# Four LayerNorm and weight-loading stages of a two-layer transformer block, with tile t's normalisation issued after tile t+1's statistics and loads issued further ahead

## The reference, cut to what matters

```
xn = layernorm(x)                                  # no weight, eps 1e-5
x  = x + L0_attn(xn) + L0_ffn(xn)                  # L0_ffn adds its own input xn, and
                                                   # begins with layernorm(xn) * norm_w + norm_b
xn = layernorm(x)
x  = x + L1_attn(xn) + L1_ffn(xn)

def L1_ffn(x):                                     # x_prev is x moved down by one token
    xr = mu_r * x + (1 - mu_r) * x_prev
    xk = mu_k * x + (1 - mu_k) * x_prev
    return sigmoid(xr @ W_r.T) * (relu(xk @ W_k.T) ** 2 @ W_v.T)
```

## Time and profile before

| what | value |
|---|---|
| time before, median of 3 runs | 15645.25 us (15638.21 to 15674.76) |
| the profiled execution's own time | 15637.75 us |
| its span, first to last instruction, slowest core | 15636.2 us |
| spans of the eight cores | 15612.7 to 15636.2 us |
| granted TensorE clock, mean of a core | 0.594 to 0.596 of full speed |
| busy: PE, ACT, DVE | 65%, 30%, 27% of the span |

### The profile page before, as it was taken

How to read it: one execution, slowest core, us unless ns; L and a number is a source line. 1 busy time by engine, 2 the same in 40 slices (tenths; PEclk the granted TensorE clock), 3 DMA queues, 4 the chain that set the end, 5 groups by cost and what they waited for, 6 DMA issues and landing times.

```text
span 15636.2 us, 129774 instructions; the slowest of 8 cores (15612.7 to 15636.2 us)
## 1 busy us (share of the span) xinstructions
...
## 2 busy tenths in 40 slices
...
DMA packets 113302, 335.26 MB, mean 21 GB/s; under 512 B 17082, under 2 KB 37115, under 8 KB 111358
## 3 DMA queue, kind: packets, MB, share of 16 engines
...
## 4 chain that ended last, share of the span: by engine, by line
PE 60%; DVE 22%; issue 8%; DMA 6%; ACT 3%; DVEq 1%; SPq 0%; ACTq 0%; POOL 0%; POOLq 0%; PEldq 0%
PE l_PS L1355 9%; PE l_PAV L1330 7%; PE l_PSM L1339 7%; PE l0a_PAV L522 5%; PE l0a_PS L541 5%; PE l0f_PS L930 3%; PE l0f_PSM L912 3%; PE l0f_PAV L901 3%; PE l0a_PQ L333 1%; DVE l0a_recip L573 1%; DVE l_recip L1387 1%; DVE l0f_rrow L956 1%; PE l_PO L1414 1%; PE l0a_PO L602 1%; DMA as_f<-f 1%
## 5 line engine op out<-in xcount | busy, mean ns | idle before, releaser
L1364 ACT ACTIVATE l_PT<-l_PS,l_cb 128x1024 bf16<-128x1024 f32 x2048 | 2281.9, 1114 | 2174.1 <-PE l_PS L1355 2160.4
L547 ACT ACTIVATE l0a_PTexp<-l0a_PS,l0a_cb 128x1024 bf16<-128x1024 f32 x1152 | 1284.6, 1115 | 1152.2 <-PE l0a_PS L541 1146.3
L1355 PE MATMUL l_PS<-l_qw,l_kT 64*128 64x512 bf16 x4096 | 1630.4, 591 | 5.8 <-DMA l_qw<-qT1f 5.8
L1330 PE MATMUL l_PAV<-l_PT,l_V 128*64 128x512 bf16 x4096 | 1309.1, 633 | 414.4 <-DVE l_PAV L1319 389.6
L939 ACT ACTIVATE l0f_PT<-l0f_PS,l0f_cb 128x1536 bf16<-128x1536 f32 (+1 forms) x704 | 1057.7, 1502 | 1124.4 <-PE l0f_PS L930 1118.3
L1339 PE MATMUL l_PSM<-l_PT,cs_onescol_bf 128*1 128x512 bf16 x4096 | 1208.9, 586 | 0.0
L522 PE MATMUL l0a_PAV<-l0a_PTexp,l0a_V 128*33 128x512 bf16 x2304 | 855.9, 586 | 540.4 <-DVE l0a_PAV L511 298.9
L1374 DVE COPY l_pavc<-l_PAV 128x512 f32<-128x512 f32 x64 | 44.3, 692 | 3695.6 <-PE l_PSM L1339 3695.6
L541 PE MATMUL l0a_PS<-l0a_qT_all,l0a_kT_all 32*128 32x512 bf16 x2304 | 913.3, 592 | 2.3 <-POOLq L98 2.3
L930 PE MATMUL l0f_PS<-l0f_qw,l0f_kTh 128*128 128x512 bf16 x2048 | 659.5, 443 | 7.1 <-DMA l0f_kTh<-kT0f 7.1
L901 PE MATMUL l0f_PAV<-l0f_PT,l0f_V 128*128 128x512 bf16 x2048 | 591.4, 398 | 48.7 <-ACT l0f_PT L939 48.1
...
...
## 6 DMA issues: line engine op xcount, KB each, us to landing
ln_x_x<-x SPq DMA_DIRECT2D x32, 512.0 KB, 3.2
a<-l0a_obuf POOLq DMA_DIRECT2D x32, 512.0 KB, 4.4
x<-x SPq DMA_DIRECT2D x32, 512.0 KB, 3.3
f<-l0f_zbuf POOLq DMA_DIRECT2D x32, 512.0 KB, 26.2
as_x<-x SPq DMA_DIRECT2D x32, 512.0 KB, 3.9
as_a<-a SPq DMA_DIRECT2D x32, 512.0 KB, 4.7
as_f<-f SPq DMA_DIRECT2D x32, 512.0 KB
x<-as_x1f POOLq DMA_DIRECT2D x32, 512.0 KB, 3.2
```

Of the source, the lines that this page charges most:

```text
L547: exp_t = b.act(lambda e, bb=bb: e.activation(PT[:, 1024 * bb:1024 * bb + 1024], PS[:, 1024 * bb:1024 * bb + 1024], AF.Exp, bias=cb[:], sc ...
L1330: b.pe(lambda e, kt=kt, g=g, ii=ii, bb=bb, last=last: e.matmul(PAV[64 * ii:64 * ii + 64, :], V1[:, 256 * kt + 64 * g:256 * kt + 64 * g + 6 ...
L1355: pe_s = b.pe(lambda e, kt=kt, v=v, ii=ii, bb=bb, qb_=qb_: e.matmul(PS[:, 1024 * bb + 512 * ii:1024 * bb + 512 * ii + 512], kT64[v][64 * i ...
L1364: exp_t = b.act(lambda e, bb=bb: e.activation(PT[:, 1024 * bb:1024 * bb + 1024], PS[:, 1024 * bb:1024 * bb + 1024], AF.Exp, bias=cb[:], sc ...
```

## The change

1. In all three LayerNorm loops the body is split in two. A step `tl` of 33 issues the load and the statistics of tile `tl` (with ACT's Ln and Exp), and then normalisation, transposes and copy-out of tile `tl - 1`. The small `mv` tile (and `rst2`, `xnf` in `emit_xn2T`) has two copies for it.
2. `emit_xn2T` has four x buffers, and a load waits for the first reader of the tile that last held the buffer.
3. `emit_assembly_ln` keeps two buffers per tensor, but a load waits for the last reader of that same buffer, two tiles before.
4. `wload` stages through four buffers (`x1s` and `a1s`) on semaphores ld4 to ld7.

No operation on data is added or removed. The core of the diff (`emit_ln_xnT` is split as the assembly is; in `emit_xn2T` the second half is the second `tensor_scalar`, the two `tensor_tensor` with weight and bias, transposes and copy-out):

```diff
 def emit_xn2T(...):
-    xs = [b.sb(f"x2_{i}", [128, D], F32, es) for i in range(2)]
-    xnf = b.sb("x2_xnf", [128, D], F32, es)
+    xs = [b.sb(f"x2_{i}", [128, D], F32, es) for i in range(4)]
+    xnfs = [b.sb(f"x2_xnf{i}", [128, D], F32, es) for i in range(2)]
...
-            waits=[("ve", ve_done)] if t >= 2 else (), slot=buf)
-        b.ve(lambda e, t=t, buf=buf: e.tensor_scalar(
-            xnf[:], xs[buf][:], stats_sb[:, 2 * t:2 * t + 1],
+                waits=[("ve", scal_hist[buf])] if t >= 4 else (), slot=buf)
+            scal_hist[buf] = b.ve(lambda e, t=t, buf=buf, nb2=nb2: e.tensor_scalar(
+                xnfs[nb2][:], xs[buf][:], stats_sb[:, 2 * t:2 * t + 1],
...
 def emit_assembly_ln(...):
-    mv = b.sb("as_mv", [128, 2], F32, es)
+    mvs = [b.sb(f"as_mv{i}", [128, 2], F32, es) for i in range(2)]
...
-    for t in range(NT):
-        buf = t % 2
-        w0 = [("ve", ve_done)] if t >= 2 else ()
+    scal_hist = [b.cnt["ve"], b.cnt["ve"]]
+    ars = {}
+    for tl in range(NT + 1):
+        if tl < NT:
+            t, buf, nb = tl, tl % 2, tl % 2
+            w0 = [("ve", scal_hist[buf])] if t >= 2 else ()
...
+            scal_hist[buf] = b.ve(lambda e, buf=buf, x1f=x1f: e.tensor_tensor(
+                x1f[:], x1f[:], xs[buf][:], OP.add), waits=[l1])
+            if add_xn:
+                scal_hist[buf] = b.ve(lambda e, t=t, buf=buf: e.tensor_scalar(
+                    tmp[:], xs[buf][:], stats_sb[:, 2 * t:2 * t + 1],
+                    stats_sb[:, 2 * t + 1:2 * t + 2], OP.subtract, OP.mult))
...
-        a_r = b.act(lambda e, t=t: e.activation(
-            stats1_sb[:, 2 * t + 1:2 * t + 2], lnv[:], AF.Exp, bias=0.0, scale=-0.5))
-        ve_done = b.ve(lambda e, t=t, x1f=x1f: e.tensor_scalar(
-            xnb[t % 2][:], x1f[:], stats1_sb[:, 2 * t:2 * t + 1],
-            stats1_sb[:, 2 * t + 1:2 * t + 2], OP.subtract, OP.mult),
-            waits=[("act", a_r), ("pe", pe_done)])
+            ars[t] = b.act(lambda e, t=t: e.activation(
+                stats1_sb[:, 2 * t + 1:2 * t + 2], lnv[:], AF.Exp, bias=0.0,
+                scale=-0.5))
+        if tl >= 1:
+            t, nb = tl - 1, (tl - 1) % 2
+            x1f = x1fs[nb]
+            ve_done = b.ve(lambda e, t=t, nb=nb, x1f=x1f: e.tensor_scalar(
+                xnb[nb][:], x1f[:], stats1_sb[:, 2 * t:2 * t + 1],
+                stats1_sb[:, 2 * t + 1:2 * t + 2], OP.subtract, OP.mult),
+                waits=[("act", ars.pop(t)), ("pe", pe_done)])
...
 def emit_l1ffn_final(...):
-    castc = [b.cnt["ve"], b.cnt["ve"]]
+    castc = [b.cnt["ve"]] * 4
+    wstages = [x1s[0], x1s[1], a1s[0], a1s[1]]
...
-            sbf = c % 2
+            sbf = c % 4
             ld = b.ld(lambda e, c=c, sbf=sbf, cap=cap: e.dma_start(
-                out=x1s[sbf][:], in_=cap[128 * c:128 * c + 128, :]),
-                waits=[("ve", castc[sbf])], slot=6 + sbf)
+                out=wstages[sbf][:], in_=cap[128 * c:128 * c + 128, :]),
+                waits=[("ve", castc[sbf])], slot=4 + sbf)
```

More of the change, by code:

```diff
@@ L162, in emit_ln_xnT @@
     st6 = b.sb(f"ln_st6_{tag}", [128, 12], F32, es)
-    mv = b.sb(f"ln_mv_{tag}", [128, 2], F32, es)
+    mvs = [b.sb(f"ln_mv{i}_{tag}", [128, 2], F32, es) for i in range(2)]
     lnv = b.sb(f"ln_lnv_{tag}", [128, 1], F32, es)
@@ L171, in emit_ln_xnT @@
             b.ve(lambda e, c=c: e.memset(xnT[c][:, 0:1], 0.0), inc="ve")
-    ve_done = b.cnt["ve"]
     pe_done = b.cnt["pe"]
@@ L176, in emit_ln_xnT @@
     scal_hist = [b.cnt["ve"]] * 4
-    for t in range(NT):
[L178 to L216, removed]
-            for c in range(NC):
[L218 to L222, removed]
@@ L635, in emit_xn2T @@
     es = b.scope()
-    xs = [b.sb(f"x2_{i}", [128, D], F32, es) for i in range(2)]
-    xnf = b.sb("x2_xnf", [128, D], F32, es)
+    xs = [b.sb(f"x2_{i}", [128, D], F32, es) for i in range(4)]
+    xnfs = [b.sb(f"x2_xnf{i}", [128, D], F32, es) for i in range(2)]
     st6 = b.sb("x2_st6", [128, 12], F32, es)
-    mv = b.sb("x2_mv", [128, 2], F32, es)
+    mvs = [b.sb(f"x2_mv{i}", [128, 2], F32, es) for i in range(2)]
     lnv = b.sb("x2_lnv", [128, 1], F32, es)
-    rst2 = b.sb("x2_rst2", [128, 1], F32, es)
+    rsts = [b.sb(f"x2_rst2{i}", [128, 1], F32, es) for i in range(2)]
     xnb = [b.sb(f"x2_xnb{i}", [128, D], BF16, es) for i in range(2)]
@@ L667, in emit_xn2T @@
     vv = b.ve(lambda e: e.tensor_copy(bbc[:], PB[:]), waits=[("pe", pv)])
-    ve_done = b.cnt["ve"]
     pe_done = b.cnt["pe"]
     evac_cnt = [b.cnt["ve"], b.cnt["ve"]]
-    for t in range(NT):
-        buf = t % 2
-        ld_t = b.ld(lambda e, t=t, buf=buf: e.dma_start(
-            out=xs[buf][:], in_=x_dram[128 * t:128 * t + 128, :]),
-            waits=[("ve", ve_done)] if t >= 2 else (), slot=buf)
-        b.ve(lambda e, t=t, buf=buf: e.tensor_scalar(
-            xnf[:], xs[buf][:], stats_sb[:, 2 * t:2 * t + 1],
[L679 to L706, removed]
@@ new lines, in emit_xn2T @@
+    scal_hist = [b.cnt["ve"]] * 4
+    ars = {}
+    for tl in range(NT + 1):
+        if tl < NT:
+            t, buf, nb2 = tl, tl % 4, tl % 2
+            ld_t = b.ld(lambda e, t=t, buf=buf: e.dma_start(
+                out=xs[buf][:], in_=x_dram[128 * t:128 * t + 128, :]),
+                waits=[("ve", scal_hist[buf])] if t >= 4 else (), slot=buf)
+            scal_hist[buf] = b.ve(lambda e, t=t, buf=buf, nb2=nb2: e.tensor_scalar(
+                xnfs[nb2][:], xs[buf][:], stats_sb[:, 2 * t:2 * t + 1],
+                stats_sb[:, 2 * t + 1:2 * t + 2], OP.subtract, OP.mult),
+                waits=[ld_t])
+            s1 = b.ve(lambda e, nb2=nb2: e.bn_stats(st6[:, 0:6], xnfs[nb2][:, 0:512]))
+            s2 = b.ve(lambda e, nb2=nb2: e.bn_stats(st6[:, 6:12], xnfs[nb2][:, 512:1024]),
+                      waits=[("ve", s1)])
+            ve_mv = b.ve(lambda e, nb2=nb2: e.bn_aggr(mvs[nb2][:], st6[:]),
+                         waits=[("ve", s2)])
+            b.act(lambda e, nb2=nb2: e.activation(lnv[:], mvs[nb2][:, 1:2], AF.Ln,
+                                                  bias=eps5[:], scale=1.0),
+                  waits=[("ve", ve_mv)])
+            ars[t] = b.act(lambda e, nb2=nb2: e.activation(
+                rsts[nb2][:], lnv[:], AF.Exp, bias=0.0, scale=-0.5))
+        if tl >= 1:
+            t, nb2 = tl - 1, (tl - 1) % 2
+            b.ve(lambda e, nb2=nb2: e.tensor_scalar(
+                xnfs[nb2][:], xnfs[nb2][:], mvs[nb2][:, 0:1], rsts[nb2][:],
+                OP.subtract, OP.mult),
+                waits=[("act", ars.pop(t))])
+            b.ve(lambda e, nb2=nb2: e.tensor_tensor(xnfs[nb2][:], xnfs[nb2][:],
+                                                    wbc[:], OP.mult))
+            ve_done = b.ve(lambda e, nb2=nb2: e.tensor_tensor(
+                xnb[nb2][:], xnfs[nb2][:], bbc[:], OP.add),
+                waits=[("pe", pe_done)])
+            pb = t % 2
+            tp = None
+            for c in range(NC):
+                w2 = [("ve", ve_done), ("ve", evac_cnt[pb])] if c == 0 else ()
+                tp = b.pe(lambda e, c=c, nb2=nb2, pb=pb: e.transpose(
+                    ptr[pb][:, 128 * c:128 * c + 128],
+                    xnb[nb2][:, 128 * c:128 * c + 128], ident[:]),
+                    waits=w2, inc="pe" if c == NC - 1 else None)
+            ov = xn2T_all.rearrange("p (c t) -> p c t", c=NC)[:, :, 128 * t:128 * t + 128]
+            evac_cnt[pb] = b.ve(lambda e, ov=ov, pb=pb: e.tensor_copy(
+                ov, ptr[pb][:].rearrange("p (c t) -> p c t", c=NC)),
+                waits=[("pe", tp)])
+            pe_done = tp
```

141 lines of the change are left out of this document (95 added, 46 removed).

## The result

The changed kernel takes 15389.87 us (median of 8 runs, 15381.4 to 15431.08), the kernel before 15648.64 us in the 8 runs beside it (15638.21 to 15674.76): a ratio of 0.9837, 95% interval 0.9827 to 0.9848. It is 258.8 us faster, 1.65%, and the interval leaves out 1. The forecast was 15382.6 us, 262.7 us less than before.

The account below looks back on a forecast made before the run. Bound: a chain through DVE with holes waiting for ACT, DMA and PE. 18.6 + 28.8 + 15.2 + 41.4 + 136.7 + 22 = 262.7 us off the median gives 15382.6 us; range 15350 to 15445.

Parts of the forecast that it names:

- The frame: LayerNorms, assembly: one chain through DVE with holes; each microsecond of hole that goes away is one off the whole.
- ACT holes: Three LayerNorm loops: normalisation no longer waits for its tile's Ln and Exp; gains 18.6, 28.8 and 15.2 us.
- Second LayerNorm, loads: Second LayerNorm: with four buffers and earlier waits, loads are ready about three tiles early; gain 41.4 us.
- Assembly, loads: Assembly: loads issued 17.5 us before need against 6.7 us taken; first tile's wait stays; gain 136.7 us.
- Weights: Last stage's weight loads: four transfers in flight keep DMA engines busy; stretch 65.2 to 43 us, gain 22 us.
- PE holes: Three LayerNorm loops: copy-outs still wait 1.44 us per tile for their transposes; nothing in the sum.
- The forecast length of the first stretch: First LayerNorm: predicted to last about 182 us in the profile after.
- That the assembly stays bound by its transfers or its two buffers: Rival, chance 0.05: transfers go on binding the assembly, its 136.7 us gain is lost; 15519 us.
- That ACT's time comes back elsewhere: Rival, chance 0.04: DVE finds Ln and Exp unfinished or pays in longer gaps; 62.6 us missing, 15445 us.
- The clock: Rival, chance 0.02: middle attention's granted clock falls from 0.85 by 0.08 or more, gain gone; at 0.50, 16570 us.
- the forecast that it keeps its length: Middle attention: all attention stages predicted to keep their length and clock; clock under 0.83 would make the prediction wrong.

Follow-up runs that it names:

- The run with the late loads: Changed kernel with second LayerNorm and assembly loads again waiting for the latest normalisation in program order; 15576.03 us (median of 4), ratio 0.9956.
- the run with two buffers: Changed kernel with two x buffers in place of four in the second LayerNorm; 15393.84 us in one run.
- The wait alone: Kernel before, only the assembly's loads now waiting for the last reader of their own buffer, loop unsplit; 15515.91 us (median of 4), ratio 0.9913.
- the version beyond the change: Changed kernel with each tile's copy-out one step later in all three LayerNorm loops; 15285.7 us (median of 4), ratio 0.9755.
- the last version: Changed kernel with copy-outs one step later, plus four staging buffers at seven more weight casts; 15227.9 us (median of 4), ratio 0.9716.
- the two built from it: Kernel before with only four weight staging buffers, 15632.16 us (one run); kernel before with only the assembly's wait edited, 15515.91 us.

## Why the prediction was right

**The frame held.** These stages are one chain through DVE, and a hole closed there came off the total: 254.6 us by the stages of the profiled executions, 258.8 by the medians of the runs.

**ACT holes.** Forecast 18.6, 28.8 and 15.2 us. The rows after leave 3.8, 3.5 and 3.5 us, so 18.1, 28.6 and 15.0 on the profiled core. I chose 0.10 us a tile for what remains; measured are 0.11 and 0.12. The run with the late loads shows that the split closes these holes by itself.

**Second LayerNorm, loads.** Forecast 41.4 us; the group went from 44.7 to 3.5, 41.2 us. That the late wait was the cause is shown by the run with two buffers. The four buffers were no part of the gain.

**Assembly, loads.** Forecast 136.7 us; 147.9 became 9.7, 138.2 us, 1.6 of it in the first tile's wait (8.1 to 6.5), which I had taken as fixed (in the later kernels that first wait is 7.0 to 7.7 us, so it varies by execution). The wait alone gave 136 us in timed runs. The tile's length of 10.5 us and the lead of 17.5 us came out at 10.49 and 17.4. The DMA share came out at 0.60, not 0.55. (Where the prediction says that tile 3's loads are not blocked by data, the loads meant are tile 2's, as the rest of its sentence says.)

**Weights.** Forecast 43 us for the stretch, measured 42.9. That it fits to 0.1 us is luck, since two errors offset one another on core 7: the rate at full share was higher than the 318 GB/s that I took (345), and the share in the stretch stayed at 0.85, so that 6.4 of the 43 us went to idle DMA engines, where I gave start and end 3 us. The first cast alone starts 3.8 us after the first issue. The Trainium skill's 358 GB/s a core ("HBM Reference", Specifications (TRN2)) lies 4% above the 345 that this trace gives at full share, and the estimate of 35 us of data that I worked out from it is nearer to 12.58 MB / 345 GB/s, 36.5 us, than mine of 39.6. With six buffers the quotient lies on both sides of that figure, 343 to 365 GB/s.

**PE holes.** They stayed, but I had put nothing for them in the sum, and together they grew from 139.2 to 142.4 us. What closes them is shown by the version beyond the change.

**What was a little too large.** The sum is 8 us above the stages' 254.6. The rows were those of the slowest core, and in three of the four stages it had more to lose than the median core: in the assembly core 7 went from 501.3 to 348.1 us, 153.2, while the median core gained 149.4; in the second LayerNorm it is 69.1 against 67.1, in the weights 22.4 against 20.8. The four stages of core 7 add up to 262.1 us, against the forecast 262.7. A sum over one core's rows is the gain of that core; I gave it to all. The forecast length of the first stretch, 182 us, does not follow from the sum either: 203.9 less 18.6 is 185.3, and 186.6 was measured.

**The rivals.** That the assembly stays bound by its transfers or its two buffers is refuted by the assembly's wait alone. The rule in the Trainium skill ("Perfetto Trace Analysis", Optimization Strategy) that a repeating gap can mean too few buffers did not apply: at L1079 the hole closed with the same two buffers, and in the second LayerNorm four buffers with late loads left it open and two with early loads closed it. That ACT's time comes back elsewhere is refuted by the rows after.

The clock: the middle attention keeps 0.85 from 6000 to 7700 us on core 7, and the kernel did not become slower. But the forecast that it keeps its length failed in the profiled execution. From the first to the last of its marks the stage lasts 3323 to 3328 us on five cores and 3306 to 3310 on the other three, where the kernel before has 3304 to 3312. This execution took 15405.51 us; less the median core's 15.4 us it comes to 15390.1, next to the 15389.87 of the eight runs. A good part of the loss lies in the inner loop, and there it goes with a lower granted clock: the row above shows 0.80 from 7519 to 7684 us on core 7. The loop, from the first to the last matmul into `l0f_PS`, lasts 2172 to 2175 us on every core before; after, it lasts 2173 to 2174 us on cores 4 and 5 and 2180 to 2192 on the other six, and these have 0.82 to 0.84 in one stretch of 550 us, cores 0 and 1 in the first, 2 and 3 in the third, 6 and 7 in the last. Of the later profiles, the one with three staging buffers and the last version have such a dip, again on neighbouring cores (4 and 5, 6 and 7), and the other four that share the change have none. The kernel before and the two built from it have none either. Three of seven against none of three is too few to say whether the change plays a part in it; what sets the dip off stays open.
